# One-hots of the sums built by ScalarE from squares, and every third gathered row added by VectorE, in a graph attention kernel

## The chip, the cores and the metric

The kernel runs on one core of one Trainium2 chip. The metric is the device time of one execution in microseconds. Before the change it was 774.21 us, the median of 3 runs (773.92 to 777.58). Engines are called PE (TensorE), DVE (VectorE), ACT (ScalarE), POOL (GpSimd) and SP (SyncE).

## The reference

One graph attention layer (GATv2), followed by a mixture-of-experts feed-forward layer. N = 1250 nodes with 256 features, 4 heads of 64, E = 40000 edges sorted by `dst`. The part that matters here:

```
xl = (x @ W_l).reshape(N, HEADS, HEAD_DIM)
xr = (x @ W_r).reshape(N, HEADS, HEAD_DIM)
e = xl[src] + xr[dst]
e = jnp.where(e >= 0, e, NEG_SLOPE * e)
score = jnp.einsum('ehd,hd->eh', e, att)
m = jax.ops.segment_max(score, dst, num_segments=N)
ex = jnp.exp(score - m[dst])
denom = jax.ops.segment_sum(ex, dst, num_segments=N)
alpha = ex / (denom[dst] + SM_EPS)
agg = jax.ops.segment_sum(alpha[:, :, None] * xl[src], dst, num_segments=N)
```

After it come bias, elu, residual and layer norm, then a router over 64 experts, the two expert matrices with a relu between them, and the weighted sum of the top two experts of each node.

## The kernel before, in words

The edges are cut into 324 items of at most 128 edges, each inside one window of 128 destination nodes. A step handles U = 3 items (u = 0, 1, 2), and there are 108 steps; a block is 9 steps (27 items), over which the softmax over destinations is computed. A node phase first computes xl and xr, writes xl to a table in HBM and prepares index tables. Then the graph phase runs `for s in range(STEPS + LAG)` on each engine, 108 + 20 steps. A route phase and an expert phase follow; the expert phase streams all expert weights from HBM.

In the graph phase a step goes like this:

- POOL gathers the 128 rows of xl of each item with an indirect DMA into a slot of the ring `G` (`gather_group`, line 131). It waits on `consumed` at first (at most 8 steps ahead) and on `freed` later, so it is at most some 5 steps ahead of TensorE.
- DVE builds the three one-hots `MT` (edge down the free dimension, node on the partitions) from the row `relb` (`build_onehot`, line 848), two steps ahead.
- PE runs `expand` for each item: with `MT` as weights it first transposes the one-hot by a matmul with `identb` into `psE[:, e, 256+8:]` (line 689), then sums xr of each edge's destination with three bf16 matmuls (line 693), then adds the gathered rows by an fp32 matmul with `ident` (line 696; fp32 runs as two passes, so two records). `psE` has two buffers.
- ACT runs `evacuate` for each item: relu of the sum from `psE` to the ring `L` (line 783), and a copy of the turned one-hot to the ring `M` (line 784), which the sum over edges uses 20 steps later.
- DVE multiplies all three items of `L` by the attention vector (`attend`, line 854) and reduces them by head to the scores `S` (`score`, line 862). `L` has 3 slots, so ACT may be up to three steps ahead of `score`.
- Twenty steps later (LAG), DVE weights the gathered rows of items 0 and 1 by alpha (`weight`, line 872), ACT those of item 2, one instruction for each head (`weigh_head`, line 805), and PE adds them up by node (`aggregate`, line 707, weights `M`).
- In between, spread over steps 2 to 7 of the next block, DVE computes the softmax of a block (`local_max`, `scan_rows`, `full_max`, `local_sum`, `full_sum`, lines 890 to 938), with small transposes on PE (lines 716 to 734) and one exponential on ACT (line 788, waited for by line 920).

The order of each engine's work is written out by hand in the loops. In iteration s DVE runs the one-hot of step s+2, the weighting of step s-18, then the softmax part if one is due, and then `attend(s-1)` and `score(s-1)`.

Of the kernel before, what the change touches and what calls it, by code (L numbers as in the profile page):

```python
# [23 lines left out]
P = 128  # L24
# [9 lines left out]
U = 3  # L34
# [107 lines left out]
def gnn_moe(nc, x, src, dst, Wl, Wr, att, bias, gamma, beta, Rw, Rb, W1, b1, W2, b2, out):  # L142
    with ExitStack() as ctx:
# [32 lines left out]
        with ExitStack() as graph:  # L176
            def gsb(name, shape, dt=F32):
                return graph.enter_context(nc.sbuf_tensor(name, shape, dt))
# [4 lines left out]
            attb = gsb("attb", [P, DX])  # L183
            identb = gsb("identb", [P, P], BF16)
            srcI = gsb("srcI", [P, NI], I32)
            G = gsb("G", [P, RG, U * DX])
            gathered = [sem(f"gathered{r}") for r in range(GS)]
# [40 lines left out]
def node_phase(nc, v):  # L228

    (x, src, dst, Wl, Wr, att, bias, gamma, beta, srcp, dstp, xl_tab, rel_d, ends_d, ident, identb, prow, iota32,  # L230
     xs, xn, xr3, attb, bg, srcI, wrow, wblk, G, M, gathered, relb, rel_in, valid, gd, ends_out, zslot, zset) = (v[k] for k in (
         "x src dst Wl Wr att bias gamma beta srcp dstp xl_tab rel_d ends_d ident identb prow iota32 "
         "xs xn xr3 attb bg srcI wrow wblk G M gathered relb rel_in valid gd ends_out zslot zset").split())
    with ExitStack() as ctx:
# [3 lines left out]
        def sem(name):  # L238
            return ctx.enter_context(nc.semaphore(name))
# [53 lines left out]
        gd_set, srcI_set = sem("gd_set"), sem("srcI_set")  # L293
        iotas, zeroed = sem("iotas"), sem("zeroed")
        rel16_set, rel_out = sem("rel16_set"), sem("rel_out")
# [36 lines left out]
        def _(act):  # L332
# [24 lines left out]
            for j in range(2):  # L357
                for i in range(NW // 2):
# [3 lines left out]
                    if j == 1:  # L362

                        act.wait_ge(xlr_sb, n + 1)
                        nc.scalar.copy(xr3_part(i, 0), xlr[:, 2 * i:2 * i + 2, 1, :]).then_inc(xr_hi, 1)

            act.wait_ge(c_in, 64)

        @block.gpsimd
        def _(g):  # L370
            nc.gpsimd.memset(pad[:, 0, :], NPAD - 1).then_inc(pad_set, 1)
            nc.gpsimd.memset(pad[:, 1, :], 0).then_inc(pad_set, 1)
            nc.gpsimd.iota(iotai[:, :], pattern=[[1, NI]], base=0, channel_multiplier=0).then_inc(iotas, 1)
            nc.gpsimd.iota(kcol_i[:, :], pattern=[[CI, CH]], base=0, channel_multiplier=1).then_inc(iotas, 1)
            nc.gpsimd.iota(pcol_i[:, :], pattern=[[P, CH]], base=0, channel_multiplier=1).then_inc(iotas, 1)
            nc.gpsimd.memset(ident[:, :], 0.0).then_inc(consts, 1)
            g.wait_ge(consts, 1)
            nc.gpsimd.affine_select(out=ident[:, :], in_=ident[:, :], compare_op=ALU.not_equal, fill=1.0, base=0,
# [18 lines left out]
        def _(pe):  # L397
            pe.wait_ge(consts, 2)

# [40 lines left out]
            for i in range(NW // 2):  # L440
                project(1, i)

        @block.vector
        def _(dve):
# [4 lines left out]
            nc.vector.memset(by_head(attb[:, :])[:, :, HD:HX], 1.0).then_inc(zeroed, 1)  # L449
            dve.wait_ge(iotas, 3)  # L450
            c(nc.vector.tensor_copy(iotak[:, :], iotai[:, :]))
# [6 lines left out]
            c(nc.vector.memset(wblk[:, :], 0))  # L458
            dve.wait_ge(consts, 2)
            c(nc.vector.tensor_copy(identb[:, :], ident[:, :]))  # L460

# [53 lines left out]
            for j in range(CH):  # L515
# [5 lines left out]
            c.then(nc.vector.tensor_tensor(valid, clampd[:, :, :], dstF[:, :, :], ALU.is_equal))  # L521
            c.then(nc.vector.scalar_tensor_tensor(out=relm[:, :, :], in0=dstF[:, :, :], scalar=1.0, in1=valid,
                                                  op0=ALU.add, op1=ALU.mult))
            nc.vector.tensor_scalar(rel16[:, :, :], relm[:, :, :], -1.0, None, ALU.add).then_inc(rel16_set, 1)
# [15 lines left out]
def graph_phase(nc, v):  # L540

    (xl_tab, rel_d, tab_d, ends_d, thr_d, ident, identb, prow, bg, xs, xn, xr3, attb, srcI, wrow, wblk, G, M, msg, gathered, relb, rel_in,
     marks, valid, gd, cut, ends_out, zslot, zset, zout, xs_d, agg) = (v[k] for k in (
         "xl_tab rel_d tab_d ends_d thr_d ident identb prow bg xs xn xr3 attb srcI wrow wblk G M msg gathered relb rel_in "
         "marks valid gd cut ends_out zslot zset zout xs_d agg").split())
    with ExitStack() as ctx:
# [3 lines left out]
        def sem(name):  # L550
            return ctx.enter_context(nc.semaphore(name))
# [21 lines left out]
        gcol = sb("gcol", [P, HEADS])  # L573
        zero = sb("zero", [P, 512], BF16)
        one = sb("one", [RB, P])
# [8 lines left out]
        dv = sem("dv_graph")  # L584
        init, rows_set, marks_out = sem("init"), sem("rows_set"), sem("marks_out")
        tab_set, tab_out, marked, ends_in = sem("tab_set"), sem("tab_out"), sem("marked"), sem("ends_in")
# [3 lines left out]
        alpha, alpha_ps, alpha_set = sem("alpha"), sem("alpha_ps"), sem("alpha_set")  # L590
        folded = sem("folded")
        block = ctx.enter_context(nc.Block())

# [84 lines left out]
        def _(pe):  # L678
            windows = [[pe.alloc_register(f"window{k}_{u}") for u in range(WPAD)] for k in range(2)]

            def expand(s, u, w):

                i, e = s * U + u, (s * U + u) % 2
                if u == 0:
                    pe.wait_ge(onehot, s + 1)
                if i >= 2:
                    pe.wait_ge(evacuated, i - 1)
                mt = MT[s % RT][:, u * P:(u + 1) * P]
                turned = nc.tensor.matmul(psE[:, e, DX:DX + P], mt, identb[:, :], start=True, stop=True)  # L689
# [47 lines left out]
            for s in range(STEPS + LAG):  # L737
# [3 lines left out]
                for u in range(U):  # L741
# [4 lines left out]
                    if (s, u) == (1, 0):  # L746
                        pe.wait_ge(init, 1)
                        for j in range(NW * D // 512):
                            nc.tensor.matmul(agg[:, j * 512:(j + 1) * 512], zero[:, 0:P], zero[:, :], start=True, stop=False,
                                             skip_group_check=True)  # L750
                    if 0 <= b < NB:
# [19 lines left out]
        def _(act):  # L771

            def evacuate(s, u):

                i, e = s * U + u, (s * U + u) % 2
                act.wait_ge(expanded, i + 1)
                if u == 0 and s >= RL:
                    act.wait_ge(scored, s - RL + 1)
                if u == 0 and s >= RM:
# [10 lines left out]
            def copy_alpha(b):  # L790
                act.wait_ge(alpha_ps, b + 1)
                if b >= 2:
# [40 lines left out]
        def _(dve):  # L833
# [3 lines left out]
            def build_onehot(s):  # L837
# [180 lines left out]
            c(V.memset(S[:, :, :, :], 0.0))  # L1018
            c(V.memset(zero[:, :], 0.0))
            dve.wait_ge(dv, c.n)  # L1020
            dve.sem_inc(init, 1)
            early = (clear_tables, mask_tables, end_tables, clear_marks, link_marks, row_marks, penalties, constants)

            for s in range(STEPS + LAG):
# [854 lines left out]
```

## Time and profile before

| | |
|---|---|
| median of 3 runs | 774.21 us |
| profiled execution, first to last instruction (no other time is given for it) | 870.6 us |
| mean granted TensorE clock | 0.913 |
| busy: PE / PE weight loads / DVE / ACT / POOL | 721.0 / 490.7 / 560.3 / 355.9 / 411.5 us |
| instructions: PE / DVE / ACT / POOL | 4151 / 1355 / 1256 / 405 |

The profiled execution took 96.4 us longer than the median run. PE's busy time is a union of records whose ends are modelled, so intervals between the starts of its instructions say more about its pace than its busy share does. A step is best read from one `attend` (line 854) to the next, since there is one in each step.

### The profile page before, as it was taken

Reading aid. Unit: us, or ns where it says so; the run is one execution under the profiler, and the core shown is the slowest. Engines: PE = TensorE matmul, PEld = TensorE weight load, DVE = VectorE, ACT = ScalarE, POOL = GpSimd, SP = SyncE. Lnnn points to the kernel's source line nnn. Section 1 sums busy time; section 2 is a strip of 40 time slices with the busy share of each in tenths; the row PEclk is TensorE's granted clock in tenths of the full one; section 3 lists DMA queues with packets and bytes.
Section 4 is the critical chain, followed back from the end, with each engine's and each line's share of the span. In section 5 each row is a group of like instructions: output and inputs, shape, how many; then the busy total and the mean of one; then the engine's idle time right before and its main releaser. Section 6 shows DMA issues by size and latency. Waiting matters only on the chain. (4 is left out here: it accounts for less than half of the span.)

```text
span 870.6 us, 14203 instructions
## 1 busy us (share of the span) xinstructions
PE 721.0 (83%) x4151; PEld 490.7 (56%) x4153; DVE 560.3 (64%) x1355; ACT 355.9 (41%) x1256; POOL 411.5 (47%) x405
## 2 busy tenths in 40 slices
PE   4844777997999889988988898998855499999995
PEld 2722444665666666666766565776544255555553
DVE  5653657886778777777876687878697333434333
ACT  1411334554455555555554464657632121121220
POOL 0566666366667656666765566710326011212121
PEclk9975798999999999999998899999955699999998
DMA  4545463344354435353534353510299899999995
GB/s 122 98 156 148 111 170 97 113 114 125 94 150 112 135 90 149 100 144 95 156 95 125 97 139 108 133 30 1 93 411 405 249 317 367 367 369 370 368 390 200
DMA packets 66875, 154.81 MB, mean 178 GB/s; under 512 B 17390, under 2 KB 30142, under 8 KB 66769
## 3 DMA queue, kind: packets, MB, share of 16 engines
q1 hardware_dynamic: 45824, 100.40, 34.2%
q0 software_dynamic: 18384, 51.06, 21.5%
q10 hardware_dynamic: 2592, 2.43, 0.9%
q8 instruction: 40, 0.66, 0.3%
q14 instruction: 35, 0.28, 0.1%
HBM read 138.76 MB, written 15.39 MB: 177 GB/s over the span
## 5 line engine op out<-in xcount | busy, mean ns | idle before, releaser
L131 POOL DMA_INDIRECT G<-xl_tab,srcI x324 | 344.6, 1064 | 196.0 <-issue 80.4
L783 ACT ACTIVATE L<-psE 128x264 f32<-128x264 f32 x324 | 126.4, 390 | 277.6 <-PE psE L696 200.0
L696 PE MATMUL psE<-G,ident 128*128 128x264 f32 x648 | 209.2, 406 | 0.0
L707 PE MATMUL agg<-msg,M 128*128 128x256 f32 x648 | 191.2, 395 | 6.4 <-issue 4.8
L693 PE MATMUL psE<-xr,MT 128*128 x972 | 176.9, 292 | 0.0
L854 DVE TENSOR_TENSOR L<-L,attb 128x792 f32<-128x792 f32 x108 | 105.7, 978 | 93.6 <-ACT M L784 46.5
L689 PE MATMUL psE<-identb,MT 128*128 128x128 bf16 x324 | 74.1, 229 | 81.4 <-issue 39.2
L805 ACT ACTIVATE msg<-G,A 128x64 f32<-128x64 f32 x432 | 136.8, 354 | 1.5 <-PE agg L707 1.2
L707 PEld LDWEIGHTS agg<-msg,M 128*128 128x128 f32 x648 | 118.5, 194 | 33.3 <-issue 17.4
L693 PEld LDWEIGHTS psE<-xr,MT 128*128 128x128 bf16 x972 | 88.5, 101 | 41.7 <-issue 6.0
L696 PEld LDWEIGHTS psE<-G,ident 128*128 128x128 f32 x648 | 105.5, 203 | 5.1
L862 DVE TENSOR_REDUCE S<-L 128x12 f32<-128x792 f32 x108 | 105.7, 978 | 3.4
L689 PEld LDWEIGHTS psE<-identb,MT 128*128 128x128 bf16 x324 | 32.7, 101 | 123.1 <-issue 65.3
L1612 POOL DMA_INDIRECT yk_d<-Y,row x33 | 31.7, 960 | 146.1 <-DVE Y L1769 133.7
L784 ACT COPY M<-psE 128x128 f32<-128x128 f32 x324 | 84.9, 262 | 0.0
L872 DVE TENSOR_TENSOR msg<-G,A 128x512 f32<-128x512 f32 x108 | 74.2, 687 | 2.5 <-PE agg L707 2.1
L1769 DVE COPY Y<-psY 128x256 f32<-128x256 f32 x32 | 13.6, 425 | 90.7 <-PE psY L1666 90.7
L1647 PE MATMUL psH<-w,xT 128*64 128x512 f32 x240 | 59.8, 620 | 0.0
L1661 PE MATMUL psY<-w,hid 128*64 128x256 f32 x480 | 57.0, 379 | 0.5 <-DMA w<-in_L_ffn_W 0.4
L1661 PEld LDWEIGHTS psY<-w,hid 128*64 128x64 f32 x480 | 34.3, 137 | 30.2 <-issue 15.4
L1828 ACT COPY hraw<-psH 128x512 f32<-128x512 f32 x33 | 19.3, 585 | 68.5 <-PE psH L1647 68.5
L1821 ACT COPY xT<-psXe 128x256 f32<-128x256 f32 x33 | 12.3, 372 | 70.8 <-PE psXe L1625 70.8
(302 smaller groups left out, 723.1 us busy)
## 6 DMA issues: line engine op xcount, KB each, us to landing
w<-in_L_ffn_W SPq DMA_DIRECT2D x120, 512.0 KB
relb<-rel_d SPq DMA_DIRECT2D x36, 288.0 KB
G<-xl_tab,srcI POOLq DMA_INDIRECT x324
tabs<-tab_d SPq DMA_DIRECT2D x48, 98.2 KB
X<-xs_d SPq DMA_DIRECT2D x58, 64.5 KB
xn<-in_L_ffn_W SPq DMA_DIRECT2D x6, 512.0 KB
h_in<-in_L_ffn_W SPq DMA_DIRECT2D x6, 512.0 KB
xs_d<-zslot SPq DMA_DIRECT2D x8, 322.5 KB
```

Source lines behind the costliest of these rows:

```text
L131: nc.gpsimd.indirect_dma_start(out=G[:, g % RG, u * DX:(u + 1) * DX], out_offset=None, in_=xl_tab, in_offset=bass.IndirectOffsetOnAxis(ap= ...
L689: turned = nc.tensor.matmul(psE[:, e, DX:DX + P], mt, identb[:, :], start=True, stop=True)
L693: nc.tensor.matmul(psE[:, e, 0:DX], mt, xr3[:, bass.ds(w * (3 * DX) + j * DX, DX)], start=(j == 0), stop=False)
L696: nc.tensor.matmul(psE[:, e, 0:DX], ident[:, :], G[:, s % RG, u * DX:(u + 1) * DX], start=False, stop=True).then_inc(expanded, 1)
L707: last = nc.tensor.matmul(agg[:, bass.ds(w * D, D)], M[:, s % RM, u * P:(u + 1) * P], msg[:, s % RA, u * D:(u + 1) * D], start=False, stop ...
L783: nc.scalar.activation(L[s % RL][:, u * DX:(u + 1) * DX], psE[:, e, 0:DX], ACT.Relu)
L784: nc.scalar.copy(M[:, s % RM, u * P:(u + 1) * P], psE[:, e, DX:DX + P]).then_inc(evacuated, 1)
L805: last = nc.scalar.activation(msg[:, s % RA, u * D + h * HD:u * D + (h + 1) * HD], G[:, s % RG, u * DX + h * HX:u * DX + h * HX + HD], ACT ...
L854: V.tensor_tensor(every, every, attb[:, :].unsqueeze(1).broadcast_to([P, U, DX]), ALU.mult).then_inc(att_mul, 1)
L862: V.tensor_reduce(S[:, b % 2, :, 1 + k * U:1 + (k + 1) * U].rearrange("p h u -> p u h"), L[s % RL][:, :].rearrange("p (u h f) -> p u h f", ...
L872: V.tensor_tensor(msg[:, s % RA, 0:n * D].rearrange("p (q d) -> p q d", d=HD), G[:, s % RG, 0:n * DX].rearrange("p (q f) -> p q f", f=HX)[ ...
L1661: last = nc.tensor.matmul(psY[part(h), b, 0:D], hid[:, b, m * P + h * CAP:m * P + (h + 1) * CAP], w2[2 * r + h][:, m, :], start=(m == 0), ...
```

## The change

For item 2 of each step PE no longer adds the gathered rows; DVE does (`add_last`), from `psE` and `G` straight into `L`, without relu. The relu of that item, and again of the other two, happens in DVE's multiplication by the attention vector, now a `scalar_tensor_tensor` (max with 0, then mult). ACT evacuates items 0 and 1 only. PE no longer turns the one-hots. Instead ACT forms them in `M`: for each item it squares `iota - rel` (`square`: 128 columns, SBUF to SBUF, bias from the new table `relc`), and a step later takes relu(1 - square) of the whole step at once (`place`: 384 columns in place). `relc` (1 minus the shifted relative index, edge on partitions, one column for each item) comes from three PE transposes and one ACT copy at the end of the node phase. Semaphores: `expand` of item 1 waits for `summed` (the add of the step before), that of items 0 and 2 for `evacuated`; `attend` waits for both.

```diff
@@ node phase, scalar
+            act.wait_ge(rel_ps, 2)
+            nc.scalar.activation(relc[:, :], psI[:, 0:NI], ACT.Copy, bias=1.0, scale=-1.0).then_inc(xlr_sb, 1)
             act.wait_ge(c_in, 64)
+            act.wait_ge(xlr_sb, NW + 1)
@@ node phase, tensor
+            pe.wait_ge(rel_set, 2)
+            for c in range(CH):
+                last = nc.tensor.transpose(psI[:, c * CI:(c + 1) * CI], relm[:, c, :], ident[0:CI, 0:CI])
+            last.then_inc(rel_ps, 1)
@@ node phase, vector
-            dve.wait_ge(consts, 2)
-            c(nc.vector.tensor_copy(identb[:, :], ident[:, :]))
@@ graph phase, tensor: expand(s, u, w)
-                if i >= 2:
-                    pe.wait_ge(evacuated, i - 1)
+                if i >= 2 and u != 1:
+                    pe.wait_ge(evacuated, s * (U - 1) + u // 2)
+                if s >= 1 and u == 1:
+                    pe.wait_ge(summed, s)
                 mt = MT[s % RT][:, u * P:(u + 1) * P]
-                turned = nc.tensor.matmul(psE[:, e, DX:DX + P], mt, identb[:, :], start=True, stop=True)
+                for j in range(3):
+                    last = nc.tensor.matmul(psE[:, e, 0:DX], mt, xr3[:, bass.ds(w * (3 * DX) + j * DX, DX)], start=(j == 0),
+                                            stop=(u == U - 1 and j == 2))
                 if u == 1:
-                    turned.then_inc(consumed, 1)
-                for j in range(3):
-                    nc.tensor.matmul(psE[:, e, 0:DX], mt, xr3[:, bass.ds(w * (3 * DX) + j * DX, DX)], start=(j == 0), stop=False)
+                    last.then_inc(consumed, 1)
                 if u == 0:
                     pe.wait_ge(gathered[s % GS], 16 * U * (s // GS + 1))
-                nc.tensor.matmul(psE[:, e, 0:DX], ident[:, :], G[:, s % RG, u * DX:(u + 1) * DX], start=False, stop=True
-                                 ).then_inc(expanded, 1)
+                if u < U - 1:
+                    last = nc.tensor.matmul(psE[:, e, 0:DX], ident[:, :], G[:, s % RG, u * DX:(u + 1) * DX], start=False, stop=True)
+                last.then_inc(expanded, 1)
@@ graph phase, scalar
-                nc.scalar.activation(L[s % RL][:, u * DX:(u + 1) * DX], psE[:, e, 0:DX], ACT.Relu)
-                nc.scalar.copy(M[:, s % RM, u * P:(u + 1) * P], psE[:, e, DX:DX + P]).then_inc(evacuated, 1)
+                nc.scalar.activation(L[s % RL][:, u * DX:(u + 1) * DX], psE[:, e, 0:DX], ACT.Relu).then_inc(evacuated, 1)
+            def square(s, u):
...
+                nc.scalar.activation(M[:, s % RM, u * P:(u + 1) * P], iota32[:, :], ACT.Square, bias=relc[:, i:i + 1]).then_inc(placed, 1)
+            def place(s):
+                act.wait_ge(placed, (U + 1) * (s + 1) - 1)
+                nc.scalar.activation(M[:, s % RM, :], M[:, s % RM, :], ACT.Relu, bias=unit[:, 0:1], scale=-1.0).then_inc(placed, 1)
...
                 for u in range(U):
+                    if s < STEPS and u < U - 1:
+                        evacuate(s, u)
+                    if u == 0 and 1 <= s <= STEPS:
+                        if s == 1:
+                            act.wait_ge(marked, 3)
+                        place(s - 1)
                     if s < STEPS:
-                        evacuate(s, u)
+                        square(s, u)
@@ graph phase, vector
+            def add_last(s):
+                u = U - 1
+                dve.wait_ge(expanded, U * (s + 1))
+                if s >= RL:
+                    dve.wait_ge(scored, s - RL + 1)
+                V.tensor_tensor(L[s % RL][:, u * DX:(u + 1) * DX], psE[:, (s * U + u) % 2, 0:DX], G[:, s % RG, u * DX:(u + 1) * DX], ALU.add
+                                ).then_inc(summed, 1)
             def attend(s):
-                dve.wait_ge(evacuated, U * (s + 1))
+                dve.wait_ge(evacuated, (U - 1) * (s + 1))
+                dve.wait_ge(summed, s + 1)
                 every = L[s % RL][:, :].rearrange("p (u f) -> p u f", u=U)
-                V.tensor_tensor(every, every, attb[:, :].unsqueeze(1).broadcast_to([P, U, DX]), ALU.mult).then_inc(att_mul, 1)
+                V.scalar_tensor_tensor(out=every, in0=every, scalar=0.0, in1=attb[:, :].unsqueeze(1).broadcast_to([P, U, DX]),
+                                       op0=ALU.max, op1=ALU.mult).then_inc(att_mul, 1)
...
                 if 1 <= s <= STEPS:
+                    add_last(s - 1)
                     attend(s - 1)
```

The PSUM of `agg` is zeroed with a 128-column tile of zeros broadcast four times instead of a 512-column one, and two semaphores are folded into others.

## Rows read from the trace of the kernel before

**Rows 1.** Windows of phases: window, us, busy (instructions) of each engine, PEclk, DMA share, GB/s.
```profile
57.00:157.00 100.00, 65.72 (x341) 41.78 (x340) 56.71 (x117) 30.43 (x112) 65.91 (x65) 0.80 0.50 137
157.00:589.00 432.00, 386.73 (x2271) 284.10 (x2272) 326.90 (x640) 232.61 (x910) 264.91 (x246) 0.97 0.42 114
...
633.00:855.00 222.00, 192.22 (x1229) 109.10 (x1227) 103.72 (x394) 47.16 (x106) 51.76 (x53) 0.87 0.97 353
```
**Rows 2.** Timeline of PE around one item of a steady step: start, us, instruction.
```profile
277.25 0.32 PE L733 MATMUL psS<-rsel,one 112*128 112x4 f32 x2
...
277.56 0.61 PE L707 MATMUL agg<-msg,M 128*128 128x256 f32 x2
278.00 0.22 PE L689 MATMUL psE<-identb,MT 128*128 128x128 bf16 x1
278.06 0.50 PE L693 MATMUL psE<-xr,MT 128*128 x3
278.40 0.61 PE L696 MATMUL psE<-G,ident 128*128 128x264 f32 x2
278.84 0.38 PE L707 MATMUL agg<-msg,M 128*128 128x256 f32 x1
```
**Rows 3.** Timeline of DVE: first and last of `full_sum`, then one step without softmax work.
```profile
271.16 0.15 DVE L926 TENSOR_TENSOR cin<-psS,tabs 112x2 f32<-112x2 f32 x1
...
274.26 0.29 DVE L938 TENSOR_TENSOR X<-X,FT 112x128 f32<-112x128 f32 x1
274.47 0.98 DVE L854 TENSOR_TENSOR L<-L,attb 128x792 f32<-128x792 f32 x1
275.48 0.98 DVE L862 TENSOR_REDUCE S<-L 128x12 f32<-128x792 f32 x1
276.38 0.31 DVE L848 TENSOR_SCALAR MT<-relb,prow 128x384 bf16<-128x384 bf16 x1
276.60 0.69 DVE L872 TENSOR_TENSOR msg<-G,A 128x512 f32<-128x512 f32 x1
277.22 0.97 DVE L854 TENSOR_TENSOR L<-L,attb 128x792 f32<-128x792 f32 x1
```
**Rows 4.** Group of the gathers: busy us, mean ns, idle before and its releasers.
```profile
L131 POOL DMA_INDIRECT G<-xl_tab,srcI x324 | 344.6, 1064 | 196.0 <-issue 80.4 <-PE agg L707 74.9 <-remote 20.8
```
**Rows 5.** Timeline of POOL, one gather straight behind another.
```profile
223.15 0.95 POOL L131 DMA_INDIRECT G<-xl_tab,srcI  x1 [0.30 <-issue]
```
**Rows 6.** Timeline of PE and ACT around one late hand-over.
```profile
280.94 0.61 PE L696 MATMUL psE<-G,ident 128*128 128x264 f32 x2
...
281.31 0.60 ACT L805 ACTIVATE msg<-G,A 128x64 f32<-128x64 f32 x2
...
283.86 0.39 ACT L783 ACTIVATE L<-psE 128x264 f32<-128x264 f32 x1 [1.96 <-PE psE L696]
...
284.15 0.26 ACT L784 COPY M<-psE 128x128 f32<-128x128 f32 x1
284.29 0.36 ACT L805 ACTIVATE msg<-G,A 128x64 f32<-128x64 f32 x1
```
**Rows 7.** Groups that stand nearest to operations which this trace does not show.
```profile
L881 DVE TENSOR_TENSOR agg<-agg,gcol 128x256 f32 x11 | 4.7, 425 | 0.8 <-PE agg L707 0.8
...
L938 DVE TENSOR_TENSOR X<-X,FT 112x128 f32<-112x128 f32 x12 | 3.5, 294 | 0.4
...
L915 DVE SCALAR_TENSOR_TENSOR X<-FT,X 112x128 f32<-112x128 f32 x12 | 3.5, 292 | 0.4
...
L813 ACT ACTIVATE xn<-xn 128x512 f32<-128x512 f32 x5 | 3.1, 620 | 0.0
...
L1847 ACT ACTIVATE w<-ident,gates 128x128 f32<-128x128 f32 x8 | 2.4, 393 | 0.0
...
L788 ACT ACT_TABLE_LOAD x1 | 1.3, 1283 | 0.0
```
**Rows 8.** Window with the longest pause of the gathers, columns as in the first group.
```profile
463.00:474.00 11.00, 9.89 (x47) 7.39 (x48) 6.83 (x12) 6.24 (x24) 3.12 (x3) 0.69 0.25 67
```

More of the change, by code:

```diff
@@ L183, in gnn_moe @@
             attb = gsb("attb", [P, DX])
-            identb = gsb("identb", [P, P], BF16)
             srcI = gsb("srcI", [P, NI], I32)
+            relc = gsb("relc", [P, NI])
             G = gsb("G", [P, RG, U * DX])
@@ L228, in node_phase @@
 def node_phase(nc, v):
[L230 to L233, printed above, removed]
+    (x, src, dst, Wl, Wr, att, bias, gamma, beta, srcp, dstp, xl_tab, rel_d, ends_d, ident, prow, iota32,
+     xs, xn, xr3, attb, bg, srcI, relc, wrow, wblk, G, M, gathered, relb, rel_in, valid, gd, ends_out, zslot, zset) = (v[k] for k in (
+         "x src dst Wl Wr att bias gamma beta srcp dstp xl_tab rel_d ends_d ident prow iota32 "
+         "xs xn xr3 attb bg srcI relc wrow wblk G M gathered relb rel_in valid gd ends_out zslot zset").split())
     with ExitStack() as ctx:
@@ L293, in node_phase @@
         gd_set, srcI_set = sem("gd_set"), sem("srcI_set")
-        iotas, zeroed = sem("iotas"), sem("zeroed")
+        zeroed = sem("zeroed")
         rel16_set, rel_out = sem("rel16_set"), sem("rel_out")
@@ L372, in _ @@
             nc.gpsimd.memset(pad[:, 1, :], 0).then_inc(pad_set, 1)
-            nc.gpsimd.iota(iotai[:, :], pattern=[[1, NI]], base=0, channel_multiplier=0).then_inc(iotas, 1)
-            nc.gpsimd.iota(kcol_i[:, :], pattern=[[CI, CH]], base=0, channel_multiplier=1).then_inc(iotas, 1)
-            nc.gpsimd.iota(pcol_i[:, :], pattern=[[P, CH]], base=0, channel_multiplier=1).then_inc(iotas, 1)
+            nc.gpsimd.iota(iotai[:, :], pattern=[[1, NI]], base=0, channel_multiplier=0).then_inc(consts, 1)
+            nc.gpsimd.iota(kcol_i[:, :], pattern=[[CI, CH]], base=0, channel_multiplier=1).then_inc(consts, 1)
+            nc.gpsimd.iota(pcol_i[:, :], pattern=[[P, CH]], base=0, channel_multiplier=1).then_inc(consts, 1)
             nc.gpsimd.memset(ident[:, :], 0.0).then_inc(consts, 1)
-            g.wait_ge(consts, 1)
+            g.wait_ge(consts, 4)
             nc.gpsimd.affine_select(out=ident[:, :], in_=ident[:, :], compare_op=ALU.not_equal, fill=1.0, base=0,
@@ L397, in _ @@
         def _(pe):
-            pe.wait_ge(consts, 2)
+            pe.wait_ge(consts, 5)
             pe.wait_ge(before_set, 1)
@@ L449, in _ @@
             nc.vector.memset(by_head(attb[:, :])[:, :, HD:HX], 1.0).then_inc(zeroed, 1)
-            dve.wait_ge(iotas, 3)
+            dve.wait_ge(consts, 3)
             c(nc.vector.tensor_copy(iotak[:, :], iotai[:, :]))
@@ L521, in _ @@
             c.then(nc.vector.tensor_tensor(valid, clampd[:, :, :], dstF[:, :, :], ALU.is_equal))
-            c.then(nc.vector.scalar_tensor_tensor(out=relm[:, :, :], in0=dstF[:, :, :], scalar=1.0, in1=valid,
-                                                  op0=ALU.add, op1=ALU.mult))
+            nc.vector.scalar_tensor_tensor(out=relm[:, :, :], in0=dstF[:, :, :], scalar=1.0, in1=valid,
+                                           op0=ALU.add, op1=ALU.mult).then_inc(rel_set, 1)
+            dve.wait_ge(rel_set, 2)
             nc.vector.tensor_scalar(rel16[:, :, :], relm[:, :, :], -1.0, None, ALU.add).then_inc(rel16_set, 1)
@@ L540, in graph_phase @@
 def graph_phase(nc, v):
-    (xl_tab, rel_d, tab_d, ends_d, thr_d, ident, identb, prow, bg, xs, xn, xr3, attb, srcI, wrow, wblk, G, M, msg, gathered, relb, rel_in,
+    (xl_tab, rel_d, tab_d, ends_d, thr_d, ident, prow, bg, xs, xn, xr3, attb, srcI, wrow, wblk, G, M, msg, gathered, relb, rel_in, iota32, relc,
      marks, valid, gd, cut, ends_out, zslot, zset, zout, xs_d, agg) = (v[k] for k in (
-         "xl_tab rel_d tab_d ends_d thr_d ident identb prow bg xs xn xr3 attb srcI wrow wblk G M msg gathered relb rel_in "
+         "xl_tab rel_d tab_d ends_d thr_d ident prow bg xs xn xr3 attb srcI wrow wblk G M msg gathered relb rel_in iota32 relc "
          "marks valid gd cut ends_out zslot zset zout xs_d agg").split())
@@ L573, in graph_phase @@
         gcol = sb("gcol", [P, HEADS])
-        zero = sb("zero", [P, 512], BF16)
+        unit = sb("unit", [P, 1])
+        zero = sb("zero", [P, P], BF16)
         one = sb("one", [RB, P])
@@ L584, in graph_phase @@
         dv = sem("dv_graph")
-        init, rows_set, marks_out = sem("init"), sem("rows_set"), sem("marks_out")
+        rows_set, marks_out = sem("rows_set"), sem("marks_out")
         tab_set, tab_out, marked, ends_in = sem("tab_set"), sem("tab_out"), sem("marked"), sem("ends_in")
@@ L591, in graph_phase @@
         folded = sem("folded")
+        placed, summed = sem("placed"), sem("summed_e")
         block = ctx.enter_context(nc.Block())
@@ L746, in _ @@
                     if (s, u) == (1, 0):
-                        pe.wait_ge(init, 1)
+                        pe.wait_ge(marked, 3)
                         for j in range(NW * D // 512):
-                            nc.tensor.matmul(agg[:, j * 512:(j + 1) * 512], zero[:, 0:P], zero[:, :], start=True, stop=False,
-                                             skip_group_check=True)
+                            nc.tensor.matmul(agg[:, j * 512:(j + 1) * 512], zero[:, :], zero[:, :].unsqueeze(1).broadcast_to([P, 512 // P, P]),
+                                             start=True, stop=False, skip_group_check=True)
                     if 0 <= b < NB:
@@ L778, in evacuate @@
                     act.wait_ge(scored, s - RL + 1)
+                nc.scalar.activation(L[s % RL][:, u * DX:(u + 1) * DX], psE[:, e, 0:DX], ACT.Relu).then_inc(evacuated, 1)
+            def square(s, u):
+                i = s * U + u
                 if u == 0 and s >= RM:
@@ L791, in copy_alpha @@
                 act.wait_ge(alpha_ps, b + 1)
+                act.wait_ge(placed, (U + 1) * GPB * (b + 1))
                 if b >= 2:
@@ L1019, in _ @@
             c(V.memset(zero[:, :], 0.0))
+            c(V.memset(unit[:, :], 1.0))
             dve.wait_ge(dv, c.n)
-            dve.sem_inc(init, 1)
+            dve.sem_inc(marked, 1)
             early = (clear_tables, mask_tables, end_tables, clear_marks, link_marks, row_marks, penalties, constants)
```

## The prediction

> **What bounds the kernel now.** I read the windows by phase first, then the timelines of PE and DVE inside the steady part, then the group of the gathers. The steady part (all engines at work, gathers and sums both running) lasts from 157 to 589 us and holds 89 of the 108 steps, so 432 / 89 = 4.85 us a step [rows 1]. What does each engine need for a step?
>
> PE: an item costs 0.06 (turning the one-hot) + 0.34 (three bf16 matmuls) + 0.44 (gathered rows, two passes) + 0.44 (aggregate) = 1.28 us from start to start [rows 2]. Three make 3.84. One item with the alpha transposes in it took 0.31 more (277.56 less 277.25 [rows 2]); with six such places in a block of 9 steps that is at most 1.9 us, or 0.2 a step. PE: 4.04 us.
>
> DVE: a step without softmax work took 2.75 us from `attend` to `attend` with no idle time [rows 3]. `full_sum` adds 3.3 us to one step (271.16 to 274.47 [rows 3]). Over all steady steps DVE is busy 326.90 / 89 = 3.67 us [rows 1]; between dependent instructions it also pauses for hundredths of a microsecond (0.03 between `attend` and its reduce [rows 3]), with some 5 such pauses a step about 0.1. DVE: 3.8 us.
>
> POOL: 0.95 + 0.30 us for a gather that waits for nothing [rows 5], 1.06 + 0.30 by the mean [rows 4]: 3.75 to 4.1 us a step. It also waited 74.9 us for `freed`, so PE holds it back more than it holds back PE. ACT: 232.61 / 89 = 2.61 us [rows 1].
>
> So PE is first at 4.04, DVE and POOL close behind. But no sum gives 4.85. The rest are holes like this: the relu at 283.86 waited 1.96 us for a matmul that ended at 281.55 and whose `expanded` signal seems to have come late, with ACT free from 281.91 on [rows 6]. The profiled execution took 870.6 us and the runs 774.2, 96.4 less. The expert phase cannot give those back: its DMA engines are 97% busy at 353 GB/s [rows 1]. If the 96.4 us come off the loop in proportion, from 57 to 589 us, a steady step of a plain run is 4.85 - 96.4 x 4.85 / 532 = 3.97 us. That fits PE's 4.04 within the error of both, and says that in plain runs the steady part runs at PE's pace with DVE at some 95% load. I take 4.04.
>
> **The change, part by part.**
>
> *PE loses work.* Three turnings (3 x 0.06 = 0.17) and one fp32 add (0.44) go: 0.61 a step [rows 2]. PE needs 3.43.
>
> *DVE gains the add.* 128x264, one operand from PSUM. The nearest row is a tensor_tensor on PSUM of 256 columns, 425 ns, against 294 for 128 columns: 1.02 ns for a column, so 433 ns [rows 7]. Since `attend` now waits for the add's own semaphore, nothing of it overlaps, and the dependent pause of 0.03 comes on top: 0.46. Bounds: 0.27 if the fixed part hid behind its neighbours (264 columns at 1.02 ns), 0.50 if one more pause is lost waiting for `expanded`. I take 0.46, the nearest row. The Trainium skill (VectorE: DVE Perf Modes, the section on the TRN2 errata) gives 120 + columns cycles of 0.96 GHz for a PSUM source, 400 ns here, against the 433 of the row; the sum below would be 3 us lower by it.
>
> *The relu in the multiplication.* A scalar_tensor_tensor of 128 columns takes 292 ns, a tensor_tensor 294 [rows 7]: nothing, and the work that it replaces is not shortened. Bounds 0 to 0.06.
>
> *ACT.* It loses one relu (0.39) and three copies (0.14 each, 284.15 to 284.29 [rows 6]) and gains three squares of 128 columns from SBUF (2.4 / 8 = 0.30 each, from the scaled copy of the same size) and one relu of 384 columns in place (at most the 0.62 of 512 columns) [rows 7]: 2.61 - 0.81 + 0.90 + 0.62 = 3.3 us. That is hidden while the step is over 3.3. Its result is needed 20 steps later, so no one waits for it.
>
> *Node phase.* Three transposes and one ACT copy (under 1 us together) lie on engines that have finished, beside DVE's splitting of xr; one identb copy less on DVE. Zero; without that cover, +1. No DMA is issued or moved, and SP's and POOL's queues stay as they were. `consumed` now comes at the end of item 1's matmuls; the first gathers feel that only where DVE is late.
>
> *The new hand-over.* PE's `expand(s, 1)` waits for `add_last(s-1)`, which stands in DVE's order behind one-hot, weighting and softmax work. Queued behind it on PE are the rest of step s, the aggregates (so `freed` and POOL) and the small transposes. From that add to the next, PE has 3.43 us of work, but DVE only needs `expand(s, 2)` of it, some 1.8 us in (0.78 + 0.44 + 0.34 and a signal of 0.24), and DVE comes back after 2.75. DVE does not wait. PE can no longer run two steps ahead through `full_sum`, but that advance is only worth something while PE is the slower one.
>
> **The sum.** DVE needs 3.8 + 0.46 = 4.26 us a step and is now first, 0.22 over PE's 4.04 of before: 89 x 0.22 = +20 us. In the 18 steps before 157 us, where tables, DMAs and gathers set the pace (100 us for 18 steps [rows 1]), I add 0.46 for a quarter of them, +2. The drain of 20 steps without `attend` and all later phases are unchanged. Against the profiled execution: 870.6 + 22 = 893, if its holes stay as they are. Against the runs: 774.2 + 22 = **796 us**. With the add at 0.27 and DVE at 3.77 the step is 4.04: no change; with 0.56 for add and relu, and 3.97 before: +0.39 x 89 = +35, 809.
>
> **The rivals.**
>
> *Faster: DVE's add falls into its waits, and what counts is PE's relief.* For it: PE is busy 90% of the steady part, DVE 76% [rows 1], and a DVE step is idle for over 1 us in this trace. If those holes were in plain runs too, a shorter PE would fill some. Against: 96 us of holes must be missing from plain runs, and holes that PE's signals make don't shrink with PE's work. It decides if DVE's step with the add stays under 4.04, that is if the add costs less than 0.24. The step then falls to POOL's pace, at the middle of its bounds 3.92: -0.12 x 89 = -11, **763 us**.
>
> *No change: POOL sets the pace on both sides.* If a gather takes 1.36 to 1.42 us in plain runs, the step is 4.1 to 4.26 before and 4.26 after, which leaves 0 to +14 us; in its lower half **776 us**. For it: the mean of 1.064 [rows 4]. Against: the 74.9 us that POOL waited for PE.
>
> *Much slower: the two engines end up in turn.* If PE, released by the add, reaches `expand(s, 2)` more than 2.75 us later, DVE waits too. Then each late signal of PE goes straight into DVE, and the pause of PE through `full_sum` and the add behind it (3.8 us) may cost it its clock: where gathers and PE stood still, the granted clock fell to 0.69 of full speed, between the levels of 1.2 and 2.4 GHz [rows 8]. One step at half rate costs 3.4 us, less DVE's cover of 0.8: 2.6 for each of 10 blocks, +26: **822 us**. The Trainium skill (TensorE: Matmul & The Clock Gate, Part 1) states that an idle PE is set back to 1.2 GHz, which speaks for this one.
>
> *Table loads.* A load takes 1.28 us, and before there is one for all 12 exponentials [rows 7]. If Square and Exp needed different tables, two loads a block would delay the exponentials and the hand-over to PE: at most 2.6 x 12 = +31 on top, **827 us**. The Trainium skill (ScalarE: Activation LUTs, Table sets) says that cheap functions are filler in every set, without naming Square; by that there would be none.
>
> **Chances.** The forecast (783 to 810) 0.54, faster 0.18, no change 0.12, in turn 0.12, table loads 0.04. Range 770 to 812: below lies most of the faster case, above it the last two. Slower by over 0.5% (about what a measurement of this kernel can tell from no change) are the forecast and the last two, 0.70; within it 0.12; faster 0.18.
>
> **What would show it.** In the profile after: item 2 on PE 0.50 us shorter and PE with idle time waiting for DVE's add; the add 0.43 us long; DVE with almost no idle time in the steady part, 3.2 us from `attend` to `attend` where there is no softmax work; POOL's waits for `freed` longer; no second table load. Wrong it would be if DVE's steady steps still had long idle times while the time fell: then DVE was not at 95% before.

## The result, and the profile after

The kernel after the change takes 793.11 us (median of 4 runs, 791.66 to 795.96); the kernel before, on the same chip, 775.89 (773.92 to 778.24). The ratio is 1.0193 [1.0147, 1.0239]: 17.2 us slower. 796 had been forecast, within 770 to 812. Some executions of a kernel are a per cent or two slower than its others, so the ratios here are of the faster runs alone, while medians are of all runs.

The profiled execution took 795.96 us with a span of 794.1, so it is one of the runs (the longest of the four). The one of before, with its 870.6 us, was not one of the 775.89: that time turned out to be what slower chips take (experiments below), and the rows before the prediction show the kernel on such a chip.

Groups of instructions of the kernel after (busy us, mean ns of one, idle time before and its releaser), for [rows 4, 7]:

```profile
L131 POOL DMA_INDIRECT G<-xl_tab,srcI x324 | 352.9, 1089 | 111.5 <-issue 95.4
L700 PE MATMUL psE<-xr,MT 128*128 x972 | 173.8, 288 | 78.8 <-DVE L L883 61.7
...
L790 ACT ACTIVATE L<-psE 128x264 f32<-128x264 f32 x216 | 84.3, 390 | 147.5 <-PE psE L707 145.4
...
L799 ACT ACTIVATE M<-iota,relc 128x128 f32<-128x128 f32 x324 | 124.5, 390 | 0.0
L891 DVE SCALAR_TENSOR_TENSOR L<-L,attb 128x792 f32<-128x792 f32 x108 | 106.3, 984 | 11.4
...
L804 ACT ACTIVATE M<-M,unit 128x384 f32<-128x384 f32 x108 | 65.4, 606 | 0.0
...
L883 DVE TENSOR_TENSOR L<-psE,G 128x264 f32<-128x264 f32 x108 | 45.2, 419 | 7.3 <-PE psE L700 6.1
```

The add takes 419 ns, the relu in the multiplication costs 6 (984 against 978). The main wait of PE is now for the add, 61.7 us, as forecast; the add itself waited 7.3 us in all, over 108 steps.

Windows of the kernel after, columns as in [rows 1]: the first 18 steps and the 89 steady ones (first, 18th and last `attend` at 57.1, 127.6 and 512.0 us).

```profile
57.00:127.00 70.00, 49.70 (x250) 28.75 (x248) 63.15 (x135) 39.52 (x109) 53.96 (x53) 0.87 0.64 171
127.00:512.00 385.00, 330.19 (x1830) 231.49 (x1829) 360.10 (x731) 279.61 (x914) 285.64 (x258) 0.98 0.49 132
```

DVE is busy 360.10 of 385 us, 94%, PE 86%, ACT 73%. A steady step is (512.0 - 127.6) / 89 = 4.32 us. But the steps fall into two kinds. Taken by nine (a block), from the 18th `attend` on, they last 39.7, 38.0, 38.0, 40.2, 38.2, 38.0, 40.3, 38.0 and 40.1 us. In the four long ones, and in no other steady steps, the granted clock of PE fell from 2.4 to 1.2 GHz for 3.4 us. One of the four falls, in windows before and in it, then the wait of PE before it and that of DVE after it:

```profile
268.00:272.60 4.60, 1.61 (x10) 0.99 (x9) 4.24 (x12) 1.62 (x5) 3.69 (x4) 1.00 0.44 117
272.70:276.00 3.30, 3.30 (x14) 2.50 (x12) 3.16 (x6) 1.55 (x7) 2.69 (x3) 0.50 0.30 82
```

```profile
271.35 0.53 PE L700 MATMUL psE<-xr,MT 128*128 x3 [2.99 <-DVE L L883]
...
283.03 0.43 DVE L883 TENSOR_TENSOR L<-psE,G 128x264 f32<-128x264 f32 x1 [1.38 <-PE psE L700]
```

So a step is 38.06 / 9 = 4.23 us where the clock stayed up, and each fall cost 1.7 to 2.2 us: 8 us in all.

Timeline of DVE through a step without softmax work of the kernel after, with two gathers and, further on, the start of PE behind a softmax part, for [rows 3, 5]:

```profile
239.62 0.42 DVE L883 TENSOR_TENSOR L<-psE,G 128x264 f32<-128x264 f32 x1
...
240.15 0.98 DVE L891 SCALAR_TENSOR_TENSOR L<-L,attb 128x792 f32<-128x792 f32 x1
...
241.16 0.98 DVE L900 TENSOR_REDUCE S<-L 128x12 f32<-128x792 f32 x1
241.16 0.95 POOL L131 DMA_INDIRECT G<-xl_tab,srcI  x1 [0.30 <-issue]
...
242.06 0.31 DVE L875 TENSOR_SCALAR MT<-relb,prow 128x384 bf16<-128x384 bf16 x1
...
242.28 0.69 DVE L910 TENSOR_TENSOR msg<-G,A 128x512 f32<-128x512 f32 x1
...
242.42 1.37 POOL L131 DMA_INDIRECT G<-xl_tab,srcI  x1 [0.30 <-issue]
...
242.88 0.43 DVE L883 TENSOR_TENSOR L<-psE,G 128x264 f32<-128x264 f32 x1
...
243.42 0.98 DVE L891 SCALAR_TENSOR_TENSOR L<-L,attb 128x792 f32<-128x792 f32 x1
...
247.32 0.43 DVE L883 TENSOR_TENSOR L<-psE,G 128x264 f32<-128x264 f32 x1
...
247.89 0.28 PE L700 MATMUL psE<-xr,MT 128*128 x1 [0.86 <-DVE L L883]
```

From `attend` to `attend` 3.27 us with nothing idle (3.21 forecast: 2.75 + 0.46). Between the start of the add and that of `attend` lie 0.53 us, 0.11 more than the add is long. From 242.88 to 247.32, 4.44 us, DVE does `local_max` as well, and PE's expand of item 1 at 247.89 has waited 0.86 us for the add.

Waits of the kernel after from 130 to 480 us (engine, line and what it waited for: us in total, times, longest):

```profile
POOL G L131 <- issue: 73.4, 241, 0.3
POOL G L131 <- PE agg L718: 4.5, 6, 1.2
...
PE psE L700 <- DVE L L883: 43.1, 40, 3.0
...
DVE L L883 <- PE psE L700: 5.3, 4, 1.5
```

PE waits for DVE, DVE hardly for PE: its four waits are one behind each fall of the clock. But POOL hardly waits either, and that was not forecast: 73.4 us are its own 0.30 between gathers, and for `freed` it waited 4.5 us where the kernel before, in its profile, waited 74.9 [rows 4].

### The profile page after: what moved, and what is told of

Its sections match the earlier page's. It is cut to its first block and busy times, and to the rows that moved or that the text cites. A ratio compares the mean times of both kernels' runs of the same rounds, so it can differ in the third digit from the quotient of the medians.

```text
span 794.1 us, 13442 instructions
## 1 busy us (share of the span) xinstructions
PE 648.7 (82%) x3615; PEld 424.1 (53%) x3616; DVE 599.6 (76%) x1463; ACT 412.4 (52%) x1257; POOL 419.7 (53%) x405
## 5 line engine op out<-in xcount | busy, mean ns | idle before, releaser
L131 POOL DMA_INDIRECT G<-xl_tab,srcI x324 | 352.9, 1089 | 111.5 <-issue 95.4
L700 PE MATMUL psE<-xr,MT 128*128 x972 | 173.8, 288 | 78.8 <-DVE L L883 61.7
L700 PEld LDWEIGHTS psE<-xr,MT 128*128 128x128 bf16 x972 | 96.3, 99 | 157.1 <-issue 115.4
L790 ACT ACTIVATE L<-psE 128x264 f32<-128x264 f32 x216 | 84.3, 390 | 147.5 <-PE psE L707 145.4
L707 PE MATMUL psE<-G,ident 128*128 128x264 f32 x432 | 138.3, 403 | 0.0
L718 PEld LDWEIGHTS agg<-msg,M 128*128 128x128 f32 x648 | 109.9, 192 | 33.3 <-issue 22.8
L799 ACT ACTIVATE M<-iota,relc 128x128 f32<-128x128 f32 x324 | 124.5, 390 | 0.0
L891 DVE SCALAR_TENSOR_TENSOR L<-L,attb 128x792 f32<-128x792 f32 x108 | 106.3, 984 | 11.4
L707 PEld LDWEIGHTS psE<-G,ident 128*128 128x128 f32 x432 | 69.7, 202 | 2.8
L804 ACT ACTIVATE M<-M,unit 128x384 f32<-128x384 f32 x108 | 65.4, 606 | 0.0
L1701 PE MATMUL psY<-w,hid 128*64 128x256 f32 x480 | 57.1, 380 | 1.4 <-DMA w<-in_L_ffn_W 1.4
L883 DVE TENSOR_TENSOR L<-psE,G 128x264 f32<-128x264 f32 x108 | 45.2, 419 | 7.3 <-PE psE L700 6.1
## 6 DMA issues: line engine op xcount, KB each, us to landing
w<-in_L_ffn_W SPq DMA_DIRECT2D x120, 512.0 KB, 14.6
xn<-in_L_ffn_W SPq DMA_DIRECT2D x6, 512.0 KB, 13.3
h_in<-in_L_ffn_W SPq DMA_DIRECT2D x6, 512.0 KB, 15.4
```

Source lines behind the costliest of these rows:

```text
L131: nc.gpsimd.indirect_dma_start(out=G[:, g % RG, u * DX:(u + 1) * DX], out_offset=None, in_=xl_tab, in_offset=bass.IndirectOffsetOnAxis(ap= ...
L700: last = nc.tensor.matmul(psE[:, e, 0:DX], mt, xr3[:, bass.ds(w * (3 * DX) + j * DX, DX)], start=(j == 0), stop=(u == U - 1 and j == 2))
L707: last = nc.tensor.matmul(psE[:, e, 0:DX], ident[:, :], G[:, s % RG, u * DX:(u + 1) * DX], start=False, stop=True)
L718: last = nc.tensor.matmul(agg[:, bass.ds(w * D, D)], M[:, s % RM, u * P:(u + 1) * P], msg[:, s % RA, u * D:(u + 1) * D], start=False, stop ...
L799: nc.scalar.activation(M[:, s % RM, u * P:(u + 1) * P], iota32[:, :], ACT.Square, bias=relc[:, i:i + 1]).then_inc(placed, 1)
L891: V.scalar_tensor_tensor(out=every, in0=every, scalar=0.0, in1=attb[:, :].unsqueeze(1).broadcast_to([P, U, DX]), op0=ALU.max, op1=ALU.mult ...
```

## The experiments

Chips differ here more than the change does, so each time is read against the kernel before on the same chip. The kernel before took 778.72 us on chip 2, and 864.32, 859.7, 862.68 and 864.49 on chips 6, 9, 14 and 15; the chip of the result has no number here. Times of a step are from `attend` to `attend`, over the 89 steady steps and over the 18 before.

**The kernel before once more (chip 6).** No edit.

> The kernel before, unchanged, for a second profile. My reading was that the first profile's steady step of 4.85 us is 4.04 plus holes that plain runs don't have. By that theory a profile whose span is near the median (774 us) shows 4.0 to 4.1 us from attend to attend over the 89 steady steps, DVE busy some 90% of the time there and PE without long waits. Rival (faster-side theory): the holes belong to the kernel, and the step stays near 4.85 with time lost elsewhere being shorter.

864.35 us against 864.32 in the other runs (23). Steps 4.79 us steady, 5.53 early, as in the first profile (4.85, 5.56). 4.0 to 4.1 had been expected. The profile of 870.6 us looks like an ordinary run of a slower chip, and my reading that 96.4 us had come with the profiled execution fell here: this profiled run is no longer than its unprofiled neighbours.

**Squares alone (chip 6).** PE adds the gathered rows of all three items and ACT evacuates them; `attend` is the old multiplication. Only the one-hots by ACT stay of the change.

```diff
-                if i >= 2 and u != 1:
-                    pe.wait_ge(evacuated, s * (U - 1) + u // 2)
-                if s >= 1 and u == 1:
-                    pe.wait_ge(summed, s)
+                if i >= 2:
+                    pe.wait_ge(evacuated, i - 1)
...
-                if u < U - 1:
-                    last = nc.tensor.matmul(psE[:, e, 0:DX], ident[:, :], ...)
+                last = nc.tensor.matmul(psE[:, e, 0:DX], ident[:, :], ...)
...
-                    add_last(s - 1)
```

> Only the first half of the change: ACT builds the one-hots from squares, PE no longer turns them, but PE still adds all gathered rows and ACT still does all three relus; DVE as before. PE's pace theory: PE 4.04 - 0.17 = 3.87 us a step, DVE 3.8, ACT some 3.6, POOL 3.75 to 4.1: 0 to 0.17 us a step less, 0.98 to 1.0 of before (760 to 776 us). If POOL sets the pace already: 1.00. If ACT's squares cost something (tables, ACT late): over 1.0, as the after kernel would then owe part of its +17 us to them.

859.85 us, ratio 0.9962 [0.9927, 0.9997]: 3 us gained of the 0.17 x 107 = 18 by which PE's work shrank. On this chip PE's pace is not the sum of its work.

**PE adds item 2 too (chip 6).** The kernel after, with the fp32 add of item 2 on PE as well; the gathered rows count twice in that item.

```diff
-                if u < U - 1:
-                    last = nc.tensor.matmul(psE[:, e, 0:DX], ident[:, :], ...)
+                last = nc.tensor.matmul(psE[:, e, 0:DX], ident[:, :], ...)
```

> The changed kernel, with PE adding the gathered rows of item 2 as well (they are then added twice, by PE and by DVE): PE gets back 0.44 us a step, 3.87 instead of 3.43. DVE's pace theory: DVE at 4.27 hides it but for a little in steps without softmax work, 0 to +0.1 us a step: 793 to 803 us. Rival, the two engines work in turn: +0.44 x 107 = +47, 840 us.

872.39 us, ratio 1.0114 [1.0061, 1.0167]. Two engines in turn would have made it some 47 us; it is 10.

**A small add (chip 6).** DVE adds 2 of the 264 columns; the rest of item 2 stays zero. The waits stay.

```diff
-                V.tensor_tensor(L[s % RL][:, u * DX:(u + 1) * DX], psE[:, ..., 0:DX], ..., ALU.add
+                V.tensor_tensor(L[s % RL][:, u * DX:u * DX + 2], psE[:, ..., 0:2], ..., ALU.add
```

> The changed kernel with DVE's add cut from 264 columns to 2 (the rest of item 2 in L is left at zero); all waits stay. DVE's pace theory: the add falls from 0.46 to some 0.2 us, DVE to 4.0 us a step, and the time by up to 0.26 x 107 = 28 us to 765, unless POOL (3.75 to 4.1 us a step) stops it at 770 to 777. Rival, hand-over sets the pace and not DVE's load: under 8 us are won.

859.11 us, ratio 0.9893 [0.9824, 0.9962]: no slower than before. The hand-over as such costs nothing here.

**The kernel after on another chip (chip 15).** No edit.

> The changed kernel, unchanged, beside the kernel before on whatever chip is given. Where the kernel before takes 774 to 778 us, both theories expect 790 to 797. On a chip where the kernel before takes some 864 us (steady step 4.79 us, with late signals from PE), the theory that DVE's load decides says that the holes leave room for the add: 0.99 to 1.01 of before; the rival, that PE and DVE now work in turn and each hole adds to DVE's load, says 4.27 + 0.75 = 5.0 us a step, +20 us, 1.02 or more.

874.5 us, ratio 1.0084 [1.0038, 1.0129]. Slower here too, by half as much, as the theory that DVE's load decides had said for such a chip. The steady step is 4.95 us. `pe_full` with 0.44 us of PE work more a step had 1.0114 on chip 6; the intervals overlap, so, chip against chip, that work cost nothing that these runs can tell.

**The add twice (chip 15).**

```diff
+                c.then(V.tensor_tensor(L[s % RL][:, u * DX:(u + 1) * DX], psE[:, (s * U + u) % 2, 0:DX],
+                                       G[:, s % RG, u * DX:(u + 1) * DX], ALU.add))
```

> The changed kernel with DVE's add made twice in every step, the second behind the first's semaphore (same result): DVE +0.46 us a step. If DVE's load is the step, +0.46 x 107 = +49 us over the changed kernel on the same chip. If DVE waits on PE or POOL a good part of the time, clearly less, under 30 us.

885.99 us, ratio 1.0254 [1.0169, 1.0339]: 11.5 us over the kernel after on the same chip, for 108 adds of 0.42 us, 45 in all. On this chip three quarters of the second add hide in waits that DVE has anyway.

**Squares alone on a chip like that of the result (chip 2).** The same kernel as squares alone.

> The half of the change without DVE's add, as squares_only, run again because that run fell on a chip where PE is held up for some 130 us in the steady part whatever the kernel. On a chip where the kernel before takes 774 to 778 us: the theory that PE sets the pace of the kernel before gives 3.87 to 3.95 us a step, 763 to 772 us, 0.985 to 0.995; if POOL sets it, 1.00. Then the whole loss of the changed kernel, and more, is owed to the add. On a chip with held-up PE: 0.99 to 1.00 again.

779.36 us against 778.72, ratio 1.002 [0.9995, 1.0045]. PE has 0.17 us less to do in each step and nothing comes of it; had PE set the pace, 763 to 772 was expected. Group and waits (130 to 480 us) of this kernel:

```profile
L131 POOL DMA_INDIRECT G<-xl_tab,srcI x324 | 350.6, 1082 | 107.9 <-issue 94.4 <-DMA xl_tab<-M 6.3 <-POOLq L234 3.5
```

```profile
POOL G L131 <- issue: 74.0, 243, 0.3
POOL G L131 <- PE agg L715: 3.3, 11, 0.3
...
PE psE L704 <- DMA G<-xl_tab,srcI: 9.9, 11, 1.7
```

POOL never waits longer than 0.3 us, and PE waits for gathered rows. 3 x (1.082 + 0.30) = 4.15 us, and the steady step is 4.195 (first, 18th and last `attend` at 56.5, 122.6 and 495.9): POOL sets the pace. By the means of nine steps, the gather of a step starts 12 to 14 us before its `attend` all through; in the kernel after that lead grows from 18 to 24 us, and past 320 us `freed` holds POOL back for the first time, so there DVE and not POOL is last. It is a near thing: gathers of 1.11 us in the steady part, with 0.30 between them, make 4.24 us a step after the change, and DVE's steps without a fall of the clock are 4.23.

**The small add on the same chip (chip 2).** The same kernel as the small add.

> As add_small (DVE's add cut to 2 columns, all waits kept). On a chip where the kernel before takes 774 to 778 us: DVE's pace theory says that DVE falls from 4.27 to 4.0 us a step and the time from 793 to 766 to 777. The rival, that the hand-over and not DVE's load costs the time, says over 785. On a chip with held-up PE: 0.985 to 1.00.

776.17 us, ratio 0.9985 [0.9955, 1.0014]. Its group of the add, and its waits from 130 to 480 us:

```profile
L883 DVE TENSOR_TENSOR L<-psE,G 128x2 f32<-128x2 f32 x108 | 16.0, 148 | 11.7 <-PE psE L700 10.0 <-PE psE L707 1.2 <-issue 0.2
```

```profile
POOL G L131 <- issue: 75.3, 247, 0.3
POOL G L131 <- PE agg L718: 1.8, 6, 0.3
...
PE psE L700 <- DVE L L883: 24.2, 17, 3.1
```

With the add 271 ns shorter (148 against 419) the whole loss is gone, and the step is 4.185 us, POOL's again. All else of the change is in this kernel: PE still waits up to 3.1 us for DVE, and the granted clock falls to 1.2 GHz for 3.4 us nine times in the steady part. Neither costs anything that shows, since DVE has time to spare. So the falls cost time only beside the full add.

**The kernel before on chip 9.** No edit.

> The kernel before, unchanged, for a profile of an execution near 775 us. Theory now: POOL sets its pace. Then POOL is idle between gathers for hardly more than its 0.3 us of issue from 130 to 480 us, waits for PE (freed) under 10 us in all, and a steady step is 4.15 to 4.22 us. By my prediction (PE's pace, 4.04) POOL would wait for PE in many places and PE would be without idle time.

861.63 us, 4.74 us a step. Another slower chip, so the step of the kernel before on a chip like that of the result stayed unmeasured.

**The kernel before with two gathers a step (chip 9).** From step 26 on the rows of item 2 are not fetched (that slot keeps old rows), so POOL has a third less to do.

```diff
-    for u in range(U):
+    for u in range(U if g < RG else U - 1):
...
-                    pe.wait_ge(gathered[s % GS], 16 * U * (s // GS + 1))
+                    pe.wait_ge(gathered[s % GS], sum(16 * (U if r < RG else U - 1) for r in range(s % GS, s + 1, GS)))
```

> The kernel before, with the gathers of item 2 left out from step 26 on (two instead of three; the slots keep old rows): POOL 2.8 instead of 4.15 us a step, all else as it was. If POOL sets the pace before, the step falls to PE's 4.04: 82 x 0.11 to 0.16 = 9 to 13 us less, 762 to 767. If PE set it, nothing, 772 to 778.

797.44 us, ratio 0.9265 [0.9203, 0.9327]. Window of this kernel, then of the kernel before on the same chip, then this kernel's group of gathers:

```profile
157.00:480.00 323.00, 322.30 (x2059) 256.33 (x2057) 293.67 (x584) 214.56 (x824) 180.17 (x156) 1.00 0.41 112
```

```profile
157.00:480.00 323.00, 293.31 (x1741) 216.23 (x1740) 251.90 (x494) 178.86 (x698) 212.10 (x200) 0.98 0.45 122
```

```profile
L131 POOL DMA_INDIRECT G<-xl_tab,srcI x242 | 266.5, 1101 | 200.4 <-PE agg L707 119.1 <-issue 52.4 <-PE psE L689 17.8
```

PE is busy for 322.30 of 323 us and POOL waits for it; the step is 4.00 us, and 3.97 to 4.02 in every block of nine. That is the 4.04 that the prediction summed for PE: without the third gather PE sets the pace.

The fall of 62 us was not foreseen (9 to 13 were, for a chip of 775 us), and POOL's own 4.1 to 4.2 us a step can't give it. On this chip PE's signals also come late, and with the third gather those late signals went from the steady part altogether (last section). So this run shows what PE alone needs, and not by itself that POOL sets the pace before.

**The kernel after with two gathers a step (chip 9).** The same omission.

> The changed kernel, with the gathers of item 2 left out from step 26 on. If DVE's load sets the pace after the change (4.22 us of work a step in a step of 4.32), the time falls by at most 82 x 0.1 = 8 us: 785 to 793. If POOL still sets it and DVE only slows POOL's gathers, it falls to that of before_two or below, under 775.

823.1 us, ratio 0.9597 [0.9512, 0.9682], where 785 to 793 had been expected for a chip of 775 us; its early steps take 5.51 us against 3.91. The steady step is 4.315, to the hundredth that of the kernel after with all its gathers on the chip of the result (4.319). The clock falls four times here too, and the blocks with a fall take 40.1 to 40.3 us (the first 38.7), the others 38.1 to 38.3. So after the change, on the chip of the result, POOL has no part in the pace.

**Squares alone with two gathers a step (chip 14).** The same omission.

> squares_only (no add on DVE, PE adds all gathered rows, no turning on PE) with the gathers of item 2 left out from step 26 on, to be compared with before_two (a steady step of 4.00 us, 797 us where the kernel before takes 860) and after_two (4.32 us, 823). Theory: with GpSimd out of the way PE's relief of 0.17 us a step shows, down to DVE's 3.8 at most: 3.83 to 3.92 us a step, 7 to 15 us under before_two, 0.910 to 0.920 of the kernel before on a chip like that. Rival: ACT's squares hold the step up, 4.0 or more.

787.38 us, ratio 0.9106 [0.9064, 0.9148]: below the 0.9265 of the kernel before with two gathers. The steady step is 3.95 against 4.00, and the early ones 5.22 against 5.74. So the squares do pay once POOL is out of the way, though in the steady part by 0.05 and not by 0.17 (3.83 to 3.92 us was expected). From 157 to 480 us PE is busy for 319.23 of 323 and DVE for 297.57; what holds the step at 3.95 was not taken apart.

No version here that does the whole work beats the kernel before; the nearest is squares alone, at no difference.

## Why the prediction was right, step by step

The time came out right; of its terms several did not, and 796 came so close by luck.

**PE, 4.04 us a step.** Right as a sum (4.00 where PE alone limits, in `before_two`). Wrong as the pace of the kernel before: the prediction's own rows gave POOL up to 4.1.

**The 96.4 us put down to the profiled execution.** This step failed. It stated that "the steady part runs at PE's pace" in plain runs, from a difference that was one of chips. On the chip of the result the pace before is, by all that the runs show, POOL's: squares alone, equal in time to the kernel before on its chip, runs at 4.195 with POOL never waiting. That was the rival "POOL sets the pace on both sides" for the side before. It was argued away with the 74.9 us that POOL waited for PE [rows 4], and those waits belong to the slower chip. The steady step of the kernel before itself was not profiled on a chip of this kind; 4.19 is inferred, and a PE and a POOL that share the limit there are not ruled out.

**DVE after the change, 3.8 + 0.46 = 4.26.** Right: 4.23 where the clock stayed up. The mean of 4.32, on the chip of the result and in `after_two`, has the falls of the clock in it. The add 419 ns for 433, with its pause 0.53 in place of 0.46, the step without softmax work 3.27 for 3.21.

**The steady sum.** The step 4.32 less 4.195 is 0.124, times 89 is +11, where 89 x 0.22 = +20 stood. The term was mis-sized, since the pace before was 4.19 and not 4.04: DVE's load is worth only 89 x 0.035 = +3, and the other 8 are the falls of the clock, which the forecast had at nothing. **The early steps**: 70.5 us for 18 after, 66.1 in squares alone, +4.4 where +2 stood. The time from the last `attend` to the end is 282.1 and 280.3 us, +1.8, and 0.6 lie before the first, both forecast at 0. 11.1 + 4.4 + 1.8 + 0.6 = 17.9, the difference of the two spans (794.1 and 776.2, one profile of each, and squares alone in the place of the kernel before); measured in medians 17.2. The forecast of +22 had +17 too much for DVE's pace and 13 too little for the clock, the early steps and the rest; that these nearly cancel is the luck.

**Relu in the multiplication, ACT, node phase.** Right: +6 ns; ACT 73% busy, its squares at 390 ns (0.30 forecast, from busy time over count; the mean in that same row was 393) and `place` at 606 (0.62) without idle time before them, both hidden.

**In turn, and the clock.** This rival happened in part. Of the ten waits behind `full_sum` (2.5 to 3.0 us each) four were followed by a fall to 1.2 GHz, DVE then waited 1.2 to 1.5 us for PE, and the block came out 2.0 us longer in the mean: 4 x 2.0 = 8 us, where the rival had 10 x 2.6 = 26. The mean granted clock of 0.98 hides it. The Trainium skill (TensorE: Matmul & The Clock Gate, Part 1) has an idle PE set back to 1.2 GHz; the trace agrees four times, and five waits just as long (2.94 to 2.99 us) were followed by no fall. Why those four, stays open.

**Table loads.** One in the loop, as before, and no second. Groups of table loads of the kernel after, of which only the second is in the graph phase:

```profile
L351 ACT ACT_TABLE_LOAD x1 | 1.3, 1283 | 9.6 <-issue 9.6
L808 ACT ACT_TABLE_LOAD x1 | 1.3, 1283 | 0.0
```

The load at L808 comes with the first exponential; from then on squares, relus and exponentials run without another. The Trainium skill (ScalarE: Activation LUTs, Table sets) says that cheap functions are in every set, without naming Square there; the trace agrees, and for Square too.

**No change.** Half right: POOL does set the pace before, by all that the runs show, but after the change DVE does, and the clock adds to it.

**Faster.** No: the add is 0.42 us, over the 0.24 at which it was to decide, and PE's relief is worth nothing where POOL sets the pace. The small add shows the same from the other side: at 148 ns the loss is gone, and nothing is gained either.

## What to carry to other kernels

Before work is taken off the engine that looks busiest, look for the engine that never waits: here it was GpSimd with three gathers of 1.08 us and 0.30 between them, at 47% busy in the page, and nothing taken from TensorE could pay. Work moved to an engine that is within a tenth of the pace counts from where it passes the pace; write down the sums of all engines, not only of the first. A hand-over that makes TensorE wait costs twice when the clock falls behind the wait, and a mean clock of 0.98 does not show that: compare the blocks of the loop with one another. And if a profile's span is far from the median, ask first whether it comes from another chip, and don't subtract the difference in proportion.

## What the runs showed of the hardware

**Chips differ by 11%, and the page hardly shows it.** The kernel before takes 776 to 779 us on two chips (perhaps one) and 860 to 864 on four others. The mean granted clock of its runs is 0.938 to 0.945 on chip 2 and 0.905 to 0.928 on the four. On the slower ones PE's signals come late, as in [rows 6]. I counted the evacuations of ACT in the steady part that began 0.6 us or more after the recorded end of their matmul, with ACT idle before them, for the items whose evacuation waits for nothing else. There were 42 in the first profile of before (93 us in all), 40 in the second (92), 44 on chip 9 (98), 40 with squares alone (90), and 12 with the kernel after on chip 15 (28), where only one item in three counts; on the chip of the result and on chip 2 none. With a third fewer gathers there were none on chip 9, before or after the change, and 6 (8 us) on chip 14; in the early steps, which still fetch all, they stay. So they come with the gathers and with the chip, not with this change. What they are stays open: nothing tried tells a late signal from a late matmul.

**The clock falls behind waits of PE.** In the steady part of the kernel after it fell four times for 3.4 us on the chip of the result and ten times, for 72 us in all, on chip 15; in the kernel before with two gathers, where PE is always busy, never. The windows around one fall on chip 15:

```profile
262.00:267.00 5.00, 2.85 (x17) 1.71 (x16) 3.19 (x7) 2.08 (x7) 3.78 (x5) 0.99 0.54 163
267.00:274.00 7.00, 4.87 (x14) 3.04 (x15) 5.86 (x16) 3.01 (x11) 4.11 (x5) 0.50 0.29 80
```

After 5 us in which PE was busy for 2.85, the granted clock was 0.50, that is 1.2 GHz, for these 7 and 3 more.

**A gather with no wait is not always 0.95 us.** Two in a row took 0.95 and 1.37 (timeline above); the mean was 1.050 to 1.101 in all kernels. At 0.95 each, three gathers would take 3.75 us a step and TensorE's 4.0 would be the limit; at the mean of 1.08 they take 4.15, and POOL is.
